# The last attention visits its heads in another order, and the last feed-forward stage runs in two halves of tokens

## Chip, cores and metric

The kernel runs on one NeuronCore of one Trainium2 chip. The metric is the device time of one execution in microseconds (us). Before the change three runs gave 1149.09, 1150.39 and 1150.68 us; the median is 1150.39 us.

## What is computed

Four sequences of 512 tokens with 256 features go through four layers:

```
L0: h = ln(x);  x1 = x + attention(h) @ Wo;  x2 = x1 + gelu(ln(x1) @ W1) @ W2
    x = x + gate * (x2 - x)                   16 heads of 16 features, causal
L1: a small adapter (256 -> 64 -> 64 -> 256), the middle weight chosen per sequence, then ln
L2: r = x + gelu(x @ Wi[e]) @ Wo[e]; x = ln(r)  weights chosen per sequence
L3: x = ln(x) * (1 + scale) + shift
    x = x + softmax(q k' / 4 + bias, masked) v @ Wo     bias: 16 x 512 x 512 per sequence
    out = x + (g * sigmoid(1.702 g)) @ W2,  g = ln(x) @ W1 + b1
```

Everything is float32, except that the scores are matmuls of bfloat16 parts.

## The kernel before

**Attentions and units.** There are eight attentions (`ATTENTIONS`, L70), each a sequence and a layer. The last one, number 7, is layer L3 of sequence 3. An attention has 64 units; a unit is one head with one tile of 128 query tokens. `unit(U)` (L521) says which: the first 32 units are heads 0 to 7 with query tiles 0, 1, 2, 3 in turn (eight units a tile), the other 32 are heads 8 to 15 with the same four tiles. Sixteen units make a batch: eight heads, two query tiles.

**Ticks.** All engines run through the same count of ticks `U`; each engine's program is a loop over ticks written out at build time. On tick U the tensor engine (PE) computes the scores of unit U (`scores`, L1402), then turns the probabilities of unit U-2 by four transposes (`turn`, L1427), and every fourth tick multiplies four turned units by the values (`values`, L1436). The vector engine (DVE) copies turned probabilities of unit U-3 out of PSUM unless the scalar engine (ACT) does (`ON_ACT`, a table that `copy_sides` at L306 makes from planned loads), and adds the bias and takes the row maximum of unit U (`maxima`, L1164, the instruction at L1178). ACT takes the exponential of unit U in place (L854), with the row sums. Sixteen units after the start of a batch the row sums are inverted (DVE, tick 17 of the batch), spread over partitions (PE, tick 21; ACT copy, tick 22, L870) and the batch's context is normalized into `ctxn` (DVE, tick 23, L1205).

**Dense stages beside attention.** Everything else is planned as events at a tick, an engine and a step (`at`, L92; `BESIDE`, L206); an engine does the events of a tick after its attention work of that tick. `plan_out` (L150) is the output projection: on PE `project` (L1306), two halves of two token tiles each, on DVE `residual` (L1126). `plan_norm` (L96) is a layer norm: `stats`, thirteen short `rsqrt` steps put between the attention work, `apply`. `block3` (L192) is the feed-forward of layer L3: `turn_tokens` (8 transposes), `feature_half` (ACT and DVE, 512 columns each), eight `hidden` steps on PE of two matmuls with 512 columns (L1326) and a gelu each on ACT (L901), then four `ff_out` steps of eight matmuls with 256 columns (L1337), `ff_add` on DVE (L1143) and the store (L915, from ACT's queue).

**The end of the kernel.** After the last attention there is nothing left to run beside. The line `[(9, norm(6), 3), (15, block3, 3)]` and `OUTPUT_AT` 8 put the projection of attention 7 at ticks 72 and 73 of it (it has units up to tick 63), the norm at 73 to 78, and the feed-forward from tick 79 on. Because heads 8 to 15 come last for every query tile, no token has all its heads before the last batch is normalized, at tick 71.

**Queues.** SP's queue issues, in the order written out, the bias loads (512 KB for two units, six pairs in a ring, L555), the weight loads, and the stacks of q and k parts (L567, L569: six transfers for eight heads; `STACKS_AT` puts those of heads 8 to 15 of attention 7 at its tick 4). GpSimd (POOL) loads and converts the mask of a query tile when its first unit is near (L830 to L836), adds the mask to a bias pair when PE has much planned beside it (`mask_sides`, L337; else PE adds it with one more matmul, L1416), and adds b2 to the residual stream (`res_l3`, L794).

Of the kernel before, what the change touches and what calls it, by code (L numbers as in the profile page):

```python
# [71 lines left out]
ALL_UNITS = UNITS * len(ATTENTIONS)  # L72
BIASED = {a: n for n, a in enumerate(a for a, (_, l) in enumerate(ATTENTIONS) if l == 1)}
# [125 lines left out]
def norm(k):  # L199
# [5 lines left out]
STACKS_AT = [(-2, 11)] + [(-28, 4)] * 2 + [(-20, 4)] + [(-28, 4)] * 3 + [(-20, 4)]  # L205
# [9 lines left out]
    [(9, norm(6), 3), (15, block3, 3)],  # L215
]
OUTPUT_AT = [None, 8, 8, 20, 8, 8, 8, 8, 8]
# [18 lines left out]

# [8 lines left out]
def plan_loads():  # L246

    ffns = sorted((first_tick("pe", "hidden", s, f), s, f) for s in range(B) for f in range(3))
    for n, (_, s, f) in enumerate(ffns):
        if n:  # L250
            _, s0, f0 = ffns[n - 1]
            at(last_tick("pe", "hidden", s0, f0) + 1, "sp", "w1", s, f)
            at(last_tick("pe", "ff_out", s0, f0) + 1, "sp", "w2", s, f)
        else:
            at(0, "sp", "w1", s, f)
            at(0, "sp", "w2", s, f)
    at(1, "sp", "expert", 0)
# [21 lines left out]
def order(engine, step, key):  # L279
# [4 lines left out]
    for _, _, k in found:  # L284
# [4 lines left out]
TURN = order("pe", "turn_tokens", lambda a: a)  # L289
NTH = {(s, k): sum(1 for x in TURN if x[1] == k and TURN[x] < n) for (s, k), n in TURN.items()}  # L290
FFN = order("pe", "hidden", lambda a: a[:2])
QKV = order("pe", "qk", lambda a: a[:2])
# [3 lines left out]
              for t0, sf in sorted((t, a[:2]) for t, e, st, a in EVENTS if e == "pe" and st == "hidden" and a[2] == 0)}  # L296
ADAPT = order("pe", "down", lambda a: a[0])
# [65 lines left out]
def build(nc, T, out):  # L363
    with ExitStack() as ctx:
# [175 lines left out]
        def res_count(s, layer):  # L540

            name, n = {0: ("res_l0", 2), 2: ("res_l2", 1), 3: ("res_l3", 1)}[layer]
            total = 0
            for _, _, step, args in sorted((t, i, st, a) for i, (t, e, st, a) in enumerate(EVENTS)
                                           if e == "p" and st.startswith("res")):
                total += NT * (2 if step == "res_l0" else 1)
                if step == name and args[0] == s:
                    return total
# [25 lines left out]
        def _(sp):  # L574
# [45 lines left out]

            def bias_first():
# [14 lines left out]
            def rows(s):  # L636
# [8 lines left out]
                for j, name in enumerate(["L2_cond_bo", "L2_cond_gamma", "L2_cond_beta"]):  # L645
# [5 lines left out]
                  "expert": expert, "rows": rows, "bias_first": bias_first}  # L651
            sp.wait_ge(idx_in, 32)
            for U in range(FIRST, LAST + 1):
# [4 lines left out]
                for step, args in steps.get(U, []):  # L658
                    do[step](*args)

        @block.gpsimd
        def _(pool):
# [136 lines left out]

            def mask_load(m):
# [24 lines left out]
            steps, do = dense_steps("p"), {"res_l0": res_l0, "res_l2": res_l2, "res_l3": res_l3}  # L826
            for U in range(FIRST, LAST + 1):

                V = U + MASK_AHEAD
                if 0 <= V < ALL_UNITS and V // UNITS in BIASED and V % 2 == 0:  # L830
                    _, _, c, t, e, j, _, _ = unit(V)
                    if c == 0 and e == 0 and j == 0:
# [11 lines left out]
        def _(act):  # L844
# [35 lines left out]

            def hi(s, l, i):
# [12 lines left out]
            def gelu(s, f, j):  # L894
# [3 lines left out]
                if f == 1 and j == 0:  # L898
# [3 lines left out]
                               bias=b1[f][:, j:j + 1]).then_inc(g_done, 1)  # L902

# [27 lines left out]
            do = {"feature_half": feature_half, "stack": lambda s, l, c: stack(act, s, l, c), "hi": hi, "mid": mid, "gelu": gelu, "down": down, "expert": expert,  # L931
# [22 lines left out]
            act.wait_ge(stored, 16 * B)  # L954
# [3 lines left out]
        def _(v):  # L958
# [70 lines left out]
            def rsqrt(s, k, i):  # L1029
# [4 lines left out]
                if i == 0:  # L1034
                    for t in range(NT):
                        count[0] += 1
                        ins = v.bn_aggr(mv[:, t, :], stats[:, t, :])
                        if t < NT - 1:
                            ins.then_inc(vec, 1)
# [59 lines left out]

            def rest_of(s, l, i):  # L1100
# [107 lines left out]
            do = {"stats": stats_of, "rsqrt": rsqrt, "apply": apply, "apply_late": apply_late,  # L1208
# [32 lines left out]
        def _(pe):  # L1241
# [27 lines left out]

            def hT_ready(s, k):  # L1270
# [35 lines left out]
            def project(s, l, i):  # L1306
                if i == 0:
# [7 lines left out]
                if i == 1:  # L1315
# [14 lines left out]
            def ff_out(s, f, t):  # L1330
                n = FFN[s, f]
# [70 lines left out]
            def scores(U):  # L1402
# [4 lines left out]
                if U == 2 * HH or U % (UNITS // 2) == 0 and U:  # L1407
# [54 lines left out]
            do = {"turn_tokens": turn_tokens, "qk": qk, "v": v_rows, "project": project, "hidden": hidden,  # L1462
# [24 lines left out]
FF_OUT_BANK = (1, 2)  # L1487
UP_BANK = (2, 0)
# [37 lines left out]
```

## Time and profile before

| what | value |
|---|---|
| median of three runs | 1150.39 us |
| the profiled execution, its own time | 1148.26 us |
| its span, first to last instruction | 1146.2 us |
| mean granted clock of PE, share of full | 0.979 |
| PE, DVE, ACT busy share of the span | 87%, 61%, 61% |

All positions below are microseconds from the span's start. The span ends at 1146.2; the profiled execution took 2.06 us more than its span. "Busy" of PE is modelled from pipelined matmuls. A float32 matmul with 256 or 512 columns leaves two records, a transpose one.

### The profile page before, as it was taken

The numbers are of one execution on the slowest core, as the hardware profiler recorded it, in microseconds if no ns is written. First come the engines' busy times: TensorE is split into PE (matmuls) and PEld (weight loads), VectorE is DVE, ScalarE is ACT, GpSimd is POOL, SyncE is SP. The second block draws the span as 40 slices with busy tenths as digits, with TensorE's granted clock in tenths as the row PEclk, the third lists the DMA queues.
The fourth block names the chain that finished last, engine by engine and source line by source line (L and its number), as shares of the span: only waits on it lengthen the run. The fifth ranks groups of instructions, "written<-read, shape, count | busy, mean of one in ns | idle before, by whom it ended". The sixth has DMA issues, their size and how long they took to land.

```text
span 1146.2 us, 22123 instructions
## 1 busy us (share of the span) xinstructions
PE 1001.6 (87%) x7746; PEld 663.6 (58%) x7834; DVE 703.7 (61%) x1964; ACT 694.9 (61%) x1608; POOL 235.7 (21%) x362
## 2 busy tenths in 40 slices
PE   4878889798889898899789899899897999899868
PEld 3445556455546566466556476566574657657545
DVE  5668773745855747945772757746738764764750
ACT  3556665673765765675665757676656775675731
POOL 8300020000320240530040000630720170080000
PEclk9889999998999999999999999999999999999989
DMA  6878425115162454854735128667385487944500
GB/s 170 222 161 199 75 74 111 39 47 102 36 140 75 90 174 129 187 200 125 143 94 113 38 93 182 206 179 195 113 204 171 139 204 234 230 138 174 176 1 18
DMA packets 118351, 154.78 MB, mean 135 GB/s; under 512 B 12956, under 2 KB 80924, under 8 KB 118244
## 3 DMA queue, kind: packets, MB, share of 16 engines
q1 hardware_dynamic: 113636, 147.04, 48.3%
q0 software_dynamic: 1936, 3.97, 1.3%
q10 hardware_dynamic: 2672, 2.36, 0.6%
q8 instruction: 64, 1.05, 0.4%
q14 instruction: 43, 0.35, 0.1%
HBM read 134.47 MB, written 18.88 MB: 134 GB/s over the span
## 4 chain that ended last, share of the span: by engine, by line
PE 54%; DVE 19%; ACT 16%; issue 10%; DMA 0%; DVEq 0%; ACTq 0%
PE bank L1337 15%; PE bank L1326 9%; PE bank L1433 8%; PE bank L1288 5%; PE bank L1447 5%; PE bank L1412 3%; DVE mrow L1169 3%; DVE bias L1178 3%; ACT gT L901 3%; ACT bias L854 3%; PE bank L1302 2%; ACT prob L851 2%; PE bank L1312 2%; ACT L901 2%; ACT pT L862 2%
## 5 line engine op out<-in xcount | busy, mean ns | idle before, releaser
L854 ACT ACTIVATE bias<-bias,mrow 128x512 f32<-128x512 f32 x256 | 184.0, 719 | 191.6 <-DVE mrow L1178 189.5
L1178 DVE CUSTOM_DVE_ANT_0 bias<-bank,bias 128x512 f32<-128x512 f32 x256 | 175.5, 687 | 195.9 <-PE bank L1412 91.6
L851 ACT ACTIVATE prob<-bank,mrow 128x128 f32<-128x128 f32 (+3 forms) x256 | 134.9, 528 | 194.6 <-DVE mrow L1169 193.1
L1169 DVE TENSOR_REDUCE mrow<-bank 128x1 f32<-128x128 f32 (+3 forms) x256 | 124.1, 486 | 169.0 <-PE bank L1418 167.8
L1433 PE MATMUL bank<-ident,bias 128*128 128x128 f32 x1024 | 157.5, 277 | 37.4 <-ACT pT L862 29.5
L1433 PEld LDWEIGHTS bank<-ident,bias 128*128 128x128 f32 x1024 | 122.2, 142 | 111.3 <-ACT bias L854 56.8
L1326 PE MATMUL bank<-hT,w 128*128 128x512 f32 x384 | 181.7, 604 | 1.3 <-ACT hT L878 1.0
L1412 PE MATMUL bank<-ks,qs 128*128 128x512 bf16 (+3 forms) x425 | 143.5, 338 | 40.1 <-ACT prob L851 34.5
L1337 PE MATMUL bank<-w,gT 128*128 128x256 f32 x768 | 174.3, 381 | 0.0
L1337 PEld LDWEIGHTS bank<-w,gT 128*128 128x128 f32 x768 | 142.5, 190 | 20.2 <-issue 2.7
L821 POOL TENSOR_TENSOR bias<-bias,negmask 128x256 f32<-128x256 f32 x180 | 118.4, 690 | 127.0 <-DMA bias<-in_fside_Bx16xSxS 124.7
L862 ACT ACTIVATE pT<-bank 128x512 f32<-128x512 f32 (+3 forms) x275 | 140.1, 509 | 0.9 <-PE bank L1433 0.9
L1186 DVE COPY pT<-bank 128x512 f32<-128x512 f32 (+3 forms) x237 | 136.3, 575 | 6.1 <-PE bank L1433 5.4
L1433 PE MATMUL bank<-ident,prob 128*128 128x128 f32 x640 | 117.2, 282 | 14.4 <-ACT pT L862 9.0
L1447 PE MATMUL bank<-pT,va 128*32 128x128 f32 x3328 | 119.2, 279 | 3.8 <-DVE ctxn L1205 2.8
L1412 PEld LDWEIGHTS bank<-ks,qs 128*128 128x128 bf16 x512 | 50.1, 98 | 117.9 <-ACT prob L851 65.0
L1326 PEld LDWEIGHTS bank<-hT,w 128*128 128x128 f32 x384 | 67.9, 193 | 60.2 <-issue 58.4
L1447 PEld LDWEIGHTS bank<-pT,va 128*32 128x32 f32 x3328 | 84.5, 110 | 25.7 <-issue 23.7
L1433 PEld LDWEIGHTS bank<-ident,prob 128*128 128x128 f32 x640 | 70.5, 144 | 39.3 <-issue 29.7
L780 POOL TENSOR_TENSOR x<-x,xy 128x256 f32<-128x256 f32 x16 | 13.0, 842 | 314.0 <-DVE h L1066 314.0
L1416 PE MATMUL bank<-negmask,identb 128*128 128x512 bf16 x165 | 62.8, 381 | 6.9 <-issue 2.2
L901 ACT ACTIVATE gT<-bank,b 128x512 f32<-128x512 f32 x96 | 60.0, 686 | 10.2 <-PE bank L1326 9.8
(157 smaller groups left out, 1136.5 us busy)
## 6 DMA issues: line engine op xcount, KB each, us to landing
bias<-in_fside_Bx16xSxS SPq DMA_DIRECT2D x128, 512.0 KB, 4.3
w<-in_L_cond_W SPq DMA_DIRECT2D x16, 1024.0 KB, 5.4
qs<-q_parts SPq DMA_DIRECT2D x30, 384.0 KB, 10.4
ks<-k_parts SPq DMA_DIRECT2D x30, 384.0 KB, 12.0
q_parts<-parts SPq DMA_DIRECT2D x80, 128.0 KB
k_parts<-parts SPq DMA_DIRECT2D x48, 128.0 KB
w<-in_L_cond_Wi SPq DMA_DIRECT2D x4, 1024.0 KB, 4.9
w<-in_L_cond_Wo SPq DMA_DIRECT2D x4, 1024.0 KB, 5.6
```

The lines of the kernel that those rows point to most:

```text
L821: pool.tensor_tensor(b_n, b_n, negmask[:, t, keys], ALU.add).then_inc(masked, 1)
L851: act.activation(prob_of(U), score_bank[U % 2][:, 0:n], ACT.Exp, bias=mrow[:, U % ROW_RING:U % ROW_RING + 1], accum_out=rsum[:, U % ROW_RI ...
L854: act.activation(prob_of(U), prob_of(U), ACT.Exp, scale=-1.0, bias=mrow[:, U % ROW_RING:U % ROW_RING + 1], accum_out=rsum[:, U % ROW_RING: ...
L862: act.activation(pT[:, U % PT_RING, 0:n // P, :], turn_bank[U % 2][:, 0:n].rearrange("p (k q) -> p k q", q=P), ACT.Identity).then_inc(pt_a, 1)
L1169: v.tensor_reduce(m, score_bank[U % 2][:, 0:n], AX_X, ALU.max, negate=True).then_inc(max_done, 1)
L1178: v.tensor_tensor_reduce(out=prob_of(U), in0=score_bank[U % 2][:], in1=prob_of(U), scale=-1.0, scalar=3e38, op0=ALU.add, op1=ALU.min, accu ...
L1186: v.tensor_copy(pT[:, U % PT_RING, 0:n // P, :], turn_bank[U % 2][:, 0:n].rearrange("p (k q) -> p k q", q=P)).then_inc(pt_v, 1)
L1326: mm = pe.matmul(dense_bank[FF_BANK[j]][:], w1[:, c, j * P:(j + 1) * P], hT[:, c, :], start=c == 0, stop=c == ND - 1)
L1337: mm = pe.matmul(dense_bank[FF_OUT_BANK[t // 2]][:, (t % 2) * D:(t % 2 + 1) * D], gT[:, j, t * P:(t + 1) * P], w2[:, j, :], start=j == 0, ...
L1412: mm = pe.matmul(score_bank[U % 2][:, 0:n], qs[:, hd, t * P:(t + 1) * P], ks[:, hd, 0:n], start=True, stop=l == 1 and not on_pe)
L1433: mm = pe.transpose(turn_bank[U % 2][:, k * P:(k + 1) * P], prob_of(U)[:, k * P:(k + 1) * P], ident[:])
L1447: mm = pe.matmul(ctx_bank[32 * j:32 * (j + 1), t % 2 * P:(t % 2 + 1) * P], v_h, pT[:, (GH * w + j) % PT_RING, k, :], start=e == 0 and k == ...
```

## The change

1. **Order of units.** In attention 7 the batches come as (heads 0-7, tiles 0-1), (heads 8-15, tiles 0-1), (heads 8-15, tiles 2-3), (heads 0-7, tiles 2-3): `LAST_ORDER`. So the token tiles 0 and 1 have all their heads after unit 31. The stack of heads 8 to 15 moves from tick 4 to tick 1, the waits for it from unit 32 to unit 16, and POOL's mask work for tiles 2 and 3 to the units 32 and 40.
2. **The last stage in halves.** `plan_half` replaces `plan_out`, `norm(6)` and `block3` for sequence 3. It runs once for token tiles 0 and 1 from tick 40 on, and once for tiles 2 and 3 from tick 72 on: `project` of the half, `residual`, `stats`, `rsqrt` with 2 instead of 4 aggregations (13 steps each time), `apply`, four transposes (`turn_half`), features of 256 columns, and eight hidden steps of two matmuls with 256 columns. Two chunks of hidden features share a PSUM bank (`HALF_BANK`).
3. **Gelus.** For the first half six hidden steps stand at ticks 50, 51, 52, 54, 55 and 56, their six gelus of 256 columns at tick 66, after the last exponential. Hidden steps 6 and 7 stand at tick 73, their gelus at 74. A gelu waits for both chunks of its bank.
4. **The end.** `last_out` writes to the two score banks and a turn bank; `ff_out` for tiles 0 and 1 stands at ticks 73 and 74, for 2 and 3 at 86 and 87. Tiles 2 and 3 are added and stored one by one. The stores of sequence 3 go through SP's queue.

```diff
+LAST_ATT = len(ATTENTIONS) - 1
+LAST_SEQ = ATTENTIONS[LAST_ATT][0]
+HALF = S // 2
+LAST_ORDER = [(0, 0), (1, 0), (1, 2), (0, 2)]
+HALF_AT = [40, 72]
...
+def plan_half(t, s, i):
+
+    at(t, "pe", "project", s, 1, i)
+    at(t + 1, "v", "residual", s, 1, i)
+    at(t + 2, "v", "stats", s, 6, i)
+    for r in range(RSQRT_STEPS):
+        at(t + 3 + r // SLOTS, f"v{r % SLOTS}", "rsqrt", s, 6, r, i)
+    at(t + 6, "v", "apply", s, 6, i)
+    at(t + 7, "p", "res_l3_half", s, i)
+    at(t + 7, "pe", "turn_half", s, i)
+    at(t + 8, "v", "feature_cols", s, i)
+    at(t + 8, "a", "feature_cols", s, i)
+    t += 10
+    ahead = (0, 0, 1, 1, 2, 2, 3, 3) if i else (0, 1, 2, 4, 5, 6, 23, 23)
+    behind = (1, 1, 2, 2, 3, 3, 4, 4) if i else (16, 16, 16, 16, 16, 16, 24, 24)
+    for j, (dt, da) in enumerate(zip(ahead, behind)):
+        at(t + dt, "pe", "hidden_cols", s, i, j)
+        at(t + da, "a", "gelu_cols", s, i, j)
+    if i == 0:
+        t = UNITS * LAST_ATT + HALF_AT[1]
+        for x in range(2):
+            at(t + 1 + x, "pe", "ff_out", s, 2, x)
+        at(t + 9, "v", "ff_add", s, 2, 0)
+        at(t + 10, "sp", "store_part", s, 0)
+    else:
+        for x in range(2):
+            at(t + 4 + x, "pe", "ff_out", s, 2, 2 + x)
+            at(t + 5 + x, "v", "ff_add", s, 2, 1 + x)
+            at(t + 6 + x, "sp", "store_part", s, 1 + x)
...
-STACKS_AT = [(-2, 11)] + [(-28, 4)] * 2 + [(-20, 4)] + [(-28, 4)] * 3 + [(-20, 4)]
+STACKS_AT = [(-2, 11)] + [(-28, 4)] * 2 + [(-20, 4)] + [(-28, 4)] * 3 + [(-20, 1)]
...
-    [(9, norm(6), 3), (15, block3, 3)],
...
-V_LOAD = {"stats": 8, "rsqrt": 2, "apply": 9, "apply_late": 9, "feature_half": 7, "rest": 8, "lo": 8, "v": 8, "residual": 14,
+V_LOAD = {"stats": 8, "rsqrt": 2, "apply": 9, "apply_late": 9, "feature_half": 7, "feature_cols": 4, "rest": 8, "lo": 8, "v": 8, "residual": 14,
...
-A_LOAD = {"feature_half": 7, "hi": 7, "mid": 7, "gelu": 10, "down": 20, "expert": 6}
+A_LOAD = {"feature_half": 7, "feature_cols": 4, "hi": 7, "mid": 7, "gelu": 10, "gelu_cols": 8, "down": 20, "expert": 6}
...
+            if a == LAST_ATT:
+                c, t = LAST_ORDER[u // BATCH][0], LAST_ORDER[u // BATCH][1] + u // (2 * GH) % 2
...
+        last_bank = [score_bank[0], score_bank[1], turn_bank[0]]
...
+            def store_part(s, i):
+                sp.wait_ge(ff_done, 2 * FFN[s, 2] + i + 1)
+                tt = LAST_TILES[i]
+                sp.dma_start(out[s].rearrange("(t p) d -> p t d", p=P)[:, tt, :], xy[s][:, tt, :]).then_inc(stored, 16)
...
+            def gelu_cols(s, i, j):
+                n, cols = FFN[s, 2], slice(HALF * i, HALF * (i + 1))
+                act.wait_ge(f1_psum, NF * (n + i) + (j | 1) + 1)
+                act.activation(gT[:, j, cols], dense_bank[HALF_BANK[j // 2]][:, j % 2 * HALF:(j % 2 + 1) * HALF], ACT.Gelu_apprx_sigmoid,
+                               bias=b1[2][:, j:j + 1]).then_inc(g_done, 1)
...
+            def turn_half(s, i):
+
+                dense_banks_free(issued)
+                pe.wait_ge(wo_done, 2 * LAST_ATT + i + 1)
+                for t in (2 * i, 2 * i + 1):
+                    pe.wait_ge(tok[5], NT * NTH[s, 5] + t + 1)
+                    for c in range(ND):
+                        mm = pe.transpose(dense_bank[c][:, t * P:(t + 1) * P], h[:, t, c * P:(c + 1) * P], ident[:])
+                mm.then_inc(t_psum, 1)
...
+            def hidden_cols(s, i, j):
+                n, cols = FFN[s, 2], slice(HALF * i, HALF * (i + 1))
+                if j == 0:
+                    pe.wait_ge(hT_a, TURN[s, 5] + 1 + i)
+                    pe.wait_ge(hT_v, TURN[s, 5] + 1 + i)
+                    pe.wait_ge(w1_in, 16 * (n + 1))
+                if j == 6:
+                    pe.wait_ge(g_done, NF * (n + i) + 2)
+                for c in range(ND):
+                    mm = pe.matmul(dense_bank[HALF_BANK[j // 2]][:, j % 2 * HALF:(j % 2 + 1) * HALF], w1[:, c, j * P:(j + 1) * P], hT[:, c, cols],
+                                   start=c == 0, stop=c == ND - 1)
+                mm.then_inc(f1_psum, 1)
+
+            def last_out(s, t):
+
+                n, i = FFN[s, 2], max(t - 1, 0)
+                if t == 0:
+                    pe.wait_ge(w2_in, 16 * (n + 1))
+                    pe.wait_ge(max_done, ALL_UNITS)
+                    copied(ALL_UNITS)
+                for j in range(NF):
+                    if t % 2 == 0:
+                        pe.wait_ge(g_done, NF * (n + t // 2) + j + 1)
+                    mm = pe.matmul(last_bank[i][:, (t == 1) * D:((t == 1) + 1) * D],
+                                   gT[:, j, t * P:(t + 1) * P], w2[:, j, :], start=j == 0, stop=j == NF - 1)
+                if t:
+                    mm.then_inc(f2_psum, 1)
...
             def project(s, l, i):
-                if i == 0:
+                if ATT[s, l] == LAST_ATT:
+                    dense_banks_free(issued)
+                    if i:
+                        pe.wait_ge(g_done, NF * FFN[s, 2] + 6)
+                    pe.wait_ge(ctx_norm, BATCHES * LAST_ATT + 2 * (i + 1))
+                elif i == 0:
...
+HALF_BANK = (2, 0, 1, 2)
+LAST_TILES = [slice(0, 2), slice(2, 3), slice(3, 4)]
```

## Rows read from the trace of the kernel before

**Rows 1.** The page: the span, and PE's busy time, share and instructions.

```profile
span 1146.2 us, 22123 instructions
PE 1001.6 (87%) x7746; PEld 663.6 (58%) x7834; DVE 703.7 (61%) x1964; ACT 694.9 (61%) x1608; POOL 235.7 (21%) x362
```

**Rows 2.** Chain that ended last, after the last attention: start us, us, what.

```profile
1099.31 0.43 DVE ctxn L1205
...
1099.88 1.98 PE bank L1312 x8
...
1101.88 0.70 DVE xy L1131
...
1109.58 1.96 PE bank L1266 x8
...
1112.47 15.75 PE bank L1326 x32
1128.22 13.83 PE bank L1337 x64
...
1142.14 0.69 DVE xy L1143
```

**Rows 3.** Windows: length, busy time (records) by engine, PEclk, DMA share, GB/s.

```profile
989.57:1010.47 20.90, 17.66 (x180) 12.53 (x182) 16.46 (x54) 13.74 (x33) 6.08 (x9) 1.00 0.92 223
1010.47:1033.05 22.58, 21.66 (x139) 11.78 (x140) 12.21 (x29) 17.35 (x30) 18.99 (x30) 1.00 0.37 115
...
1053.25:1093.79 40.54, 35.04 (x401) 24.45 (x406) 30.62 (x84) 29.99 (x77) 0.00 (x0) 1.00 0.59 186
...
1099.74:1146.20 46.46, 35.19 (x120) 23.35 (x120) 10.09 (x31) 7.56 (x10) 2.77 (x4) 0.89 0.03 12
...
1105.00:1106.00 1.00, 0.00 (x0) 0.00 (x0) 0.97 (x3) 0.00 (x0) 0.00 (x0) 0.91 0.00 0
1106.00:1107.00 1.00, 0.00 (x0) 0.00 (x0) 0.90 (x7) 0.00 (x0) 0.00 (x0) 0.50 0.00 0
...
1116.00:1117.00 1.00, 1.00 (x4) 0.50 (x3) 0.00 (x0) 0.69 (x1) 0.00 (x0) 0.97 0.00 0
```

**Rows 4.** Line L1178 in 1053.2:1094.2: ns min/median/max, first and last start.

```profile
L1178 DVE CUSTOM_DVE_ANT_0 bias<-bank,bias x31: 678/684/692, 1053.2 to 1093.8; 128x512 f32<-128x512 f32 x31
```

**Rows 5.** Timeline of DVE, attention 7, maxima of units 9, 10 and 11.

```profile
993.27 0.69 DVE L1178 CUSTOM_DVE_ANT_0 bias<-bank,bias 128x512 f32<-128x512 f32 x1 [3.01 <-PE bank L1416]
...
996.00 0.67 DVE L1178 CUSTOM_DVE_ANT_0 bias<-bank,bias 128x512 f32<-128x512 f32 x1
...
999.33 0.68 DVE L1178 CUSTOM_DVE_ANT_0 bias<-bank,bias 128x512 f32<-128x512 f32 x1
```

**Rows 6.** Timeline of ACT and PE: a gelu group, then the attention's end.

```profile
1015.59 1.28 ACT L901 ACT_TABLE_LOAD   x1
1016.88 1.85 ACT L901 ACTIVATE gT<-bank,b 128x512 f32<-128x512 f32 x3
...
1095.23 0.58 ACT L862 ACTIVATE pT<-bank 128x512 f32<-128x512 f32 x1
...
1096.66 0.60 ACT L862 ACTIVATE pT<-bank 128x512 f32<-128x512 f32 x1 [0.86 <-PE bank L1433]
...
1098.89 0.38 ACT L870 ACTIVATE spread<-bank 128x256 f32<-128x256 f32 x1 [1.63 <-PE bank L1458]
...
1099.88 3.69 PE L1312 MATMUL bank<-wo,ctxn 128*128 128x256 f32 x16 [1.02 <-DVE ctxn L1205]
...
1111.56 0.78 ACT L878 ACTIVATE hT<-bank,norm_all 128x512 f32<-128x512 f32 x1 [12.29 <-PE bank L1266]
```

**Rows 7.** DMA issues near 987 and at the end: count, KB, us to landing.

```profile
bias<-in_fside_Bx16xSxS SPq DMA_DIRECT2D x1, 512.0 KB, 14.2
ks<-k_parts SPq DMA_DIRECT2D x1, 384.0 KB, 12.4
...
out<-xy ACTq DMA_DIRECT2D x1, 512.0 KB, 2.9
```

More of the change, by code:

```diff
@@ L246, in plan_loads @@
 def plan_loads():
-    ffns = sorted((first_tick("pe", "hidden", s, f), s, f) for s in range(B) for f in range(3))
+    ffns = sorted((first_tick("pe", "hidden_cols" if (s, f) == (LAST_SEQ, 2) else "hidden", *((s,) if (s, f) == (LAST_SEQ, 2) else (s, f))), s, f)
+                  for s in range(B) for f in range(3))
     for n, (_, s, f) in enumerate(ffns):
@@ L289 @@
 TURN = order("pe", "turn_tokens", lambda a: a)
+TURN[LAST_SEQ, 5] = len(TURN)
 NTH = {(s, k): sum(1 for x in TURN if x[1] == k and TURN[x] < n) for (s, k), n in TURN.items()}
+NTH[LAST_SEQ, 5] = sum(1 for x in TURN if x[1] == 5) - 1
 FFN = order("pe", "hidden", lambda a: a[:2])
+FFN[LAST_SEQ, 2] = len(FFN)
 QKV = order("pe", "qk", lambda a: a[:2])
@@ L545, in res_count @@
                                            if e == "p" and st.startswith("res")):
-                total += NT * (2 if step == "res_l0" else 1)
+                total += {"res_l0": 2 * NT, "res_l3_half": NT // 2}.get(step, NT)
                 if step == name and args[0] == s:
+                    return total
+                if step == "res_l3_half" and (s, layer) == (LAST_SEQ, 3) and args[1] == half:
                     return total
@@ L799, in res_l3, with res_l3_half @@
                 res_landed()
+            def res_l3_half(s, i):
+                pool.wait_ge(tok[5], NT * NTH[s, 5] + 2 * (i + 1))
+                for t in (2 * i, 2 * i + 1):
+                    res(pool.tensor_tensor(xy[s][:, t, :], xy[s][:, t, :], b2[1][:], ALU.add))
+                res_landed()
             def mask_load(m):
@@ L830, in _ @@
                 if 0 <= V < ALL_UNITS and V // UNITS in BIASED and V % 2 == 0:
-                    _, _, c, t, e, j, _, _ = unit(V)
-                    if c == 0 and e == 0 and j == 0:
+                    a, _, c, t, e, j, _, _ = unit(V)
+                    if e == 0 and j == 0 and (c, t) in ([(0, 0), (0, 1), (1, 2), (1, 3)] if a == LAST_ATT else [(0, x) for x in range(NT)]):
                         if BIASED[V // UNITS]:
@@ L1027, in _, with rsqrt @@
             chain = [0]
-            def rsqrt(s, k, i):
+            def rsqrt(s, k, i, half=None):
                 var, bits, guess, sq = nwt[:, 0, :], nwt[:, 1, :], rstd, nwt[:, 2, :]
@@ L1034, in rsqrt @@
                 if i == 0:
-                    for t in range(NT):
+                    tiles = range(NT) if half is None else range(2 * half, 2 * half + 2)
+                    for t in tiles:
                         count[0] += 1
                         ins = v.bn_aggr(mv[:, t, :], stats[:, t, :])
-                        if t < NT - 1:
+                        if t < tiles[-1]:
                             ins.then_inc(vec, 1)
@@ L1207, in _ @@
             steps = dense_steps("v")
-            do = {"stats": stats_of, "rsqrt": rsqrt, "apply": apply, "apply_late": apply_late,
+            do = {"stats": stats_of, "feature_cols": feature_cols, "rsqrt": rsqrt, "apply": apply, "apply_late": apply_late,
                   "feature_half": feature_half, "rest": rest_of, "lo": lo, "v": values_out, "residual": residual,
```

45 lines of the change are left out of this document (33 added, 12 removed).

## The prediction

> **What bounds the kernel now.** I read the page first: PE is busy 87% of the span [rows 1], so in most of the kernel PE time is kernel time. Then the chain of waits from its end backwards, because the change touches only attention 7 and what follows. It shows a tail: the last context is normalized at 1099.74, and the kernel ends at 1146.2, 46.46 us later, in which nothing runs beside anything [rows 2, 3]. Three things stand in that tail one behind the other: PE's own work (projection, turn, hidden 15.75, output 13.83), a stretch of DVE alone from the first residual (1101.88) to the turn (1109.58), and the store. PE is busy 35.19 of the 46.46 us. The clock is in it too: PE works until 1103.57 (3.69 from 1099.88 [rows 6]), idles for DVE until 1109.58, and its granted clock goes from 1.00 to 0.50 in that gap and is back only at 1116 [rows 3]: the lower level, 1.2 instead of 2.4 GHz.
>
> Next, the windows by stage in attention 7, to learn what work costs when it is put beside attention. Undisturbed, from 1053.25 to 1093.79, 31 maxima start, that is 30 ticks in 40.54 us: 1.35 us a tick [rows 3, 4]. PE is busy 35.04 of it, DVE 30.62, ACT 29.99: PE idles 0.18 us a tick and no engine is full; what sets the tick is the round of scores, maximum, exponential, turn. Ticks 8 to 17 carry a whole projection, norm and turn of another sequence: 20.90 us for 10 ticks, 7.4 over 13.5. Ticks 18 to 26 carry eight whole hidden steps with eight gelus: 22.58 us for 9, 10.4 over 12.2 [rows 3].
>
> **The tail after the change.** I build it from the last normalization. Matmuls with 256 columns: 64 records of L1337 in 13.83 us, two records each, 0.432 us a matmul [rows 2].
> - wait for `ctxn` 0.14 (1099.74 to 1099.88 [rows 2]);
> - projection of the second half, 4 matmuls: half of 3.69, 1.85 [rows 6];
> - hidden steps 6 and 7 of the first half, 4 matmuls: 1.73;
> - output of tiles 0 and 1, 16 matmuls: 6.91. Beside these 8.6 us DVE does the second half's residual, norm and apply. Before, both halves took 7.7 (1101.88 to 1109.58 [rows 2]); one half is less than that, so it is ready and its stall is gone. Gelus 6 and 7 have six matmuls (2.6 us) to hide behind;
> - turn of the half, 4 transposes: 8 took 1.96 at the 0.50 clock [rows 2, 3], so 0.5, taken 0.6 with the start;
> - features of 256 columns: a stall of PE. 512 columns took 0.78, the 256-column copy 0.38 [rows 6]; 0.5 plus 0.15 to pass it on, 0.65;
> - eight hidden steps, 16 matmuls: 6.91; gelus follow pair by pair on an otherwise free ACT;
> - output of tiles 2 and 3, 16 matmuls: 6.91;
> - add of 256 columns: 0.5 with its waits (0.69 for 512, 0.43 for the normalization's 256 [rows 2]);
> - store: 3.37 now, from 1142.83 to 1146.2, with 2.9 to landing for 512 KB [rows 2, 7]. A quarter of the bytes: between 1 and 3.4, taken 2.3. Tiles 0 to 2 are stored under matmuls.
>
> Sum 28.5. The clock should stay at 1.00 in all of it, as PE has work without a long pause.
>
> In front of it stands ACT's new batch: one table load and six gelus at tick 66, before the spread copy of tick 70, which releases the last normalization. In the old kernel ACT made copies at 1095.23 and 1096.66 and the spread copy at 1098.89 to 1099.27 [rows 6]. With the planned load of the gelus, `copy_sides` gives the very last copy to DVE (worked through from its formula: 14 of the copies from unit 38 on change sides, unit 63 among them), so ACT is free at 1095.8. Table load 1.28; three gelus of 512 columns took 1.85 [rows 6], 0.6 each, so six of 256 lie between 1.8 and 3.7; with 0.38 each, 2.3. End 1099.4, the spread copy 0.5 later than before; with the upper end and a last copy still on ACT it would be 3.4. I take 0.6. DVE's copy of unit 63 costs 0.1, within it.
>
> - Norm part, ticks 40 to 48. From the old ticks 8 to 10 [rows 3, 5]: the tick with one projection half lasted 3.70, so 2.35 over; the tick with residual and stats of one half (996.00 to 999.33) 3.33, 1.98 over, of which I take 1.7 since the copies there go to ACT. The rsqrt ticks were no longer than others (7.4 less ticks 8 to 10's 5.7 leaves 1.7 for rsqrt, apply of four tiles, turn and features). Half of that last is 0.85, less what slack takes back: 0.2. Sum 4.2. Bounds: half of the whole stage, 3.7, and the whole, 7.4.
> - Hidden part, ticks 50 to 56. The old stage cost 10.4 for 16 matmuls of 0.86, 13.8 us of PE: 0.76 per us of PE. 0.76 x 5.2 = 3.9. PE's idle time of 0.18 x 7 ticks says the same (5.2 - 1.3). There are no gelus and no table loads beside it, which speaks for less: lower bound 2; upper, six eighths of 10.4, 7.8.
> - Masks: the planner's table of PE loads doesn't know the new steps, so PE keeps its mask matmuls in these ticks; that is the state of the undisturbed ticks and adds nothing.
> - The stack of heads 8-15 goes out some 5.7 us earlier. Its last transfer took 12.4 us to land [rows 7]; it is wanted at unit 16, some 28 us after tick 1. What it pushes back is bias loads: the first behind the stack took 14.2 instead of the usual 4 [rows 7]; that one will be the pair of units 10 and 11, issued at about 981.7 and landed at 995.9, wanted at 996.00 [rows 5]. Between 0 and 2; 0.5.
> - POOL's mask work and `res_l3_half` have a free engine; the first half's weights come as before: 0.
>
> Sum 8.6. **Net 17.4 - 8.6 = 8.8 us less.** The profiled execution would go from 1148.26 to 1139.5 (span 1137.4). It lies 2.1 below the median of the runs; from that median, 1150.39, the forecast is **1141.6 us**.
>
> **Rivals.**
> 1. *Attention swallows more.* PE idles 0.18 us a tick; over the 18 ticks 40 to 57 that is 3.2 of the 7.6 us added. Then attention pays 4.4 rather than 8.1, and the time is 1137.9. For it: no gelus beside the hidden steps. Against: the old stages cost 0.76 per us of PE and DVE is loaded as well.
> 2. *The gelu batch holds the spread copy, and the clock falls in the gap.* With 3.4 rather than 0.6 PE would stand from 1098.86 to about 1103.3. The old gap of 6 us cost the clock 6.5 us at half speed after its end (1109.58 to 1116), 3.2 us of work [rows 2, 3]. Together 6.0: 1147.6. The Trainium skill (TensorE: Matmul & The Clock Gate, "Why this matters for your kernels") warns against idle gaps between matmul bursts; the trace agrees for the 6 us gap, and shows a full clock across the 1.0 us one before 1099.88. Against: the last copy leaves ACT.
> 3. *Slower: each stop costs its worst.* The mechanism is that PE works its ticks in order: a dense piece between turn and next scores delays both units in flight, whatever its columns. Eight pieces (projection, turn, six hidden) at the worst measured, 2.35, are 18.8; with residual and stats at 1.98, 20.8, and the time is 1150.39 + 20.8 - 17.4 = 1153.8. It decides once ticks 40 to 63 last over 31.1 + 17.4 = 48.5 us. Against: whole hidden steps with 1.7 us of PE cost only 1.3 each on average.
> 4. *The change doesn't do what it says:* the first half isn't through by tick 63, since each step waits for the one before across engines, and PE stands in front of a wait. The distance of apply and turn is one tick, as in the old norm, which worked in ticks 8 to 17. If the six hidden steps waited instead of filling, about their 5.2 us would come back: 1146.8.
>
> **How the numbers follow.** The forecast 0.63, its own range 1138.5 to 1145; rival 1, 0.12; rival 2, 0.11; rival 3, 0.05; rival 4, 0.05; 0.04 for a sum that cancels (attention at both its upper bounds, 15.2 us: 1148.7). Leaving out rival 3 and part of 1 and 2, the range is 1136.8 to 1147.2. A difference under 0.2% (2.3 us) can't be told from none in this kernel; only rival 3 is over 1152.7, and the cancelling sum with part of rival 3 lies within. Faster 0.91, same 0.05, slower 0.04.
>
> **What would show it.** In the profile after: from the last `ctxn` to the end some 28.5 us with the clock at 1.00; one table load in ACT's last batch, the spread copy within 1 us of the last transposes of the sums; ticks 40 to 63 in some 39 us (31.1 + 8.1); the first maximum of unit 10 waiting little; no wait of PE at the second turn. The forecast is wrong if the ticks with one short hidden step last over 2.4 us each, if PE waits over 3 us for the last `ctxn`, or if the clock falls after 1095.

## The result and the profile after

The changed kernel takes 1140.5 us (median of four runs, 1138.92 to 1140.99) against 1150.54 for the kernel before, measured beside it: 10.0 us less, ratio 0.9911, interval 0.9894 to 0.9929. The forecast was 1141.6. The profiled execution took 1140.81 us, its span is 1138.7.

The page of the kernel after, the line that answers to [rows 1]: PE's work is the same, its share a little higher.

```profile
PE 1001.3 (88%) x7778; PEld 669.2 (59%) x7866; DVE 704.7 (62%) x1975; ACT 698.0 (61%) x1620; POOL 235.3 (21%) x362
```

Windows of the kernel after, in the columns of [rows 3]: ticks 8 to 18, 40 to 50, 50 to 58 of attention 7 (from the maximum of one unit to that of another), and the last normalization to the end.

```profile
991.11:1013.95 22.84, 18.18 (x181) 12.58 (x183) 17.44 (x54) 13.88 (x33) 7.31 (x12) 1.00 0.78 213
1065.09:1082.66 17.57, 15.61 (x171) 11.18 (x173) 13.23 (x47) 13.19 (x32) 1.42 (x2) 1.00 0.54 167
1082.66:1096.94 14.28, 14.17 (x135) 10.85 (x137) 8.15 (x22) 8.28 (x20) 0.00 (x0) 1.00 0.33 109
1110.13:1138.70 28.57, 25.09 (x116) 21.61 (x116) 7.08 (x24) 4.76 (x11) 1.41 (x2) 1.00 0.06 19
```

The first and the last row answer to rows of [rows 3]: 20.90 has become 22.84, 46.46 has become 28.57, and the clock of the tail 1.00 instead of 0.89. The whole difference of the two spans, taken from the starts of the maxima:

| stretch | before | after | difference |
|---|---|---|---|
| start to attention 7, unit 0 | 978.90 | 980.44 | +1.54 |
| ticks 0 to 8 | 10.67 | 10.67 | 0 |
| ticks 8 to 18 | 20.90 | 22.84 | +1.94 |
| ticks 18 to 40 | 51.42 | 51.14 | -0.28 |
| ticks 40 to 50 | 14.78 | 17.57 | +2.79 |
| ticks 50 to 58 | 10.64 | 14.28 | +3.64 |
| ticks 58 to 63 | 6.48 | 6.81 | +0.33 |
| maximum of unit 63 to end of last normalization | 5.94 | 6.36 | +0.42 |
| last normalization to end | 46.47 | 28.59 | -17.88 |
| span | 1146.2 | 1138.7 | -7.5 |

The first line is not the change's: up to attention 7 the plan is the same, and over all profiles of this study unit 0 starts between 978.1 and 983.6. Without it the two profiles differ by 9.0 us, as the medians roughly do. So from here on the stages are compared rather than spans. From tick 40 on, a stage that an edit doesn't touch repeats to 0.1 us where the clock is the same. Ticks 8 to 18 don't repeat when the stack goes out at tick 1: they took 22.16 to 24.32 us in the eight profiles of such kernels, against 20.22 to 20.90 in the five with the stack at tick 4.

The chain of waits of the kernel after, its last 33 us (start us, us, what), where [rows 2] showed the old tail:

```profile
1105.79 1.28 ACT L975
...
1107.46 1.93 ACT gT L975 x5
1109.38 0.28 ACT spread L932
1109.67 0.02 issue
1109.69 0.44 DVE ctxn L1289
1110.13 0.14 issue
1110.26 1.97 PE bank L1440 x8
1112.23 1.73 PE bank L1374 x8
1113.95 6.91 PE bank L1388 x32
1120.86 0.45 PE bank L1361 x4
1121.31 0.02 issue
1121.34 0.57 ACT hT L946
1121.91 0.07 issue
1121.98 7.14 PE bank L1374 x32
1129.13 6.92 PE bank L1388 x32
...
1136.17 0.42 DVE xy L1227
```

DVE's norm has vanished from the chain: it runs from 1112.3 to 1117.9 beside PE's work. One table load and the gelus stand right in front of the spread copy. From 1110.26 to 1136.05 the chain is PE but for the 0.7 us of the features; the last add and the store follow.

### The profile page after: what moved, and what is told of

Read it like the earlier page. It is cut to its first block, busy times and chain, and to the rows that moved or that the text cites. A ratio compares the mean times of both kernels' runs of the same rounds, so it can differ in the third digit from the quotient of the medians.

```text
span 1138.7 us, 22222 instructions
## 1 busy us (share of the span) xinstructions
PE 1001.3 (88%) x7778; PEld 669.2 (59%) x7866; DVE 704.7 (62%) x1975; ACT 698.0 (61%) x1620; POOL 235.3 (21%) x362
## 4 chain that ended last, share of the span: by engine, by line
PE 54%; DVE 18%; ACT 16%; issue 10%; DMA 2%; POOL 1%; ACTq 0%; DVEq 0%; POOLq 0%
PE bank L1467 14%; PE bank L1563 8%; PE bank L1454 7%; PE bank L1577 5%; PE bank L1411 5%; PE bank L1542 3%; DVE mrow L1253 3%; DVE bias L1262 3%; ACT gT L969 3%; ACT bias L916 3%; PE bank L1425 2%; ACT prob L913 2%; PE bank L1440 2%; ACT L969 2%; PE bank L1546 2%
## 5 line engine op out<-in xcount | busy, mean ns | idle before, releaser
L1454 PE MATMUL bank<-hT,w 128*128 128x512 f32 x352 | 166.3, 600 | 0.7 <-issue 0.6
L1467 PE MATMUL bank<-w,gT 128*128 128x256 f32 x704 | 160.4, 381 | 0.0
L1467 PEld LDWEIGHTS bank<-w,gT 128*128 128x128 f32 x704 | 130.3, 190 | 18.1 <-issue 2.2
L1454 PEld LDWEIGHTS bank<-hT,w 128*128 128x128 f32 x352 | 61.3, 192 | 51.1 <-issue 50.7
L1548 PE MATMUL bank<-causal,identb 128*128 128x128 bf16 x256 | 57.4, 225 | 2.5 <-ACT prob L913 1.1
```

The lines of the kernel that those rows point to most:

```text
L1454: mm = pe.matmul(dense_bank[FF_BANK[j]][:], w1[:, c, j * P:(j + 1) * P], hT[:, c, :], start=c == 0, stop=c == ND - 1)
L1467: mm = pe.matmul(dense_bank[FF_OUT_BANK[t // 2]][:, (t % 2) * D:(t % 2 + 1) * D], gT[:, j, t * P:(t + 1) * P], w2[:, j, :], start=j == 0, ...
```

## The experiments

Most are the changed kernel with one edit. The first is the kernel before with one part of the change, and halves_after, best and best_mask have several edits. `...` in a diff marks what is left out. The times of one kernel scatter by several us (the six of stack_tick4 lie between 1136.12 and 1144.54), so a difference of medians below some 3 us is no evidence by itself; what an edit does is read from the stages.

**order_only.** The kernel before, with `LAST_ORDER` in `unit` and `normalize`, the early stack, and POOL's masks.

```diff
+LAST_ORDER = [(0, 0), (1, 0), (1, 2), (0, 2)]
-... + [(-20, 4)]
+... + [(-20, 1)]
+            if a == LAST_ATT:
+                c, t = LAST_ORDER[u // BATCH][0], LAST_ORDER[u // BATCH][1] + u // (2 * GH) % 2
...
```

> The kernel before with nothing of the change but the order of units in attention 7, the stack of heads 8-15 at tick 1 and POOL's mask work moved with it; the old tail stays. Theory: the order itself costs nothing, the early stack pushes bias loads back, so ticks 9 to 17 of attention 7 take 1.7 us more than before, as they do in the changed kernel; total +1.7 us. Rival: those 1.7 us come from something else in the changed kernel (its plan of copies, code layout); then attention 7 lasts as long as before and the time is the same.

Measured: 1152.34 us, ratio 1.0027 (1.0010 to 1.0043) to the kernel before. Its window of ticks 8 to 18, and DVE's maximum of unit 10 in its timeline with the idle time before it:

```profile
991.45:1014.36 22.91, 18.21 (x181) 12.61 (x183) 17.43 (x53) 13.88 (x33) 7.33 (x12) 1.00 0.75 211
```

```profile
999.01 0.69 DVE L1182 CUSTOM_DVE_ANT_0 bias<-bank,bias 128x512 f32<-128x512 f32 x1 [1.04 <-DMA bias<-in_fside_Bx16xSxS]
```

The order by itself costs nothing (ticks 40 to 50 take 14.80, 50 to 58 take 10.64, as before); ticks 8 to 18 take 2.0 us more, of which 0.3 comes back by tick 40 (51.13 instead of 51.42 for ticks 18 to 40). That leaves the expected 1.7. DVE waits for the bias of unit 10, and that transfer took 15.5 us to land. This run has the order and the early stack together; the next one tells them apart.

**stack_tick4.**

```diff
-STACKS_AT = ... + [(-20, 1)]
+STACKS_AT = ... + [(-20, 4)]
```

> The changed kernel with the stack of heads 8-15 of attention 7 back at tick 4. Theory: bias loads of units 8 to 13 are out before it, the wait for the bias of unit 10 (0.95 us) goes, and the stack still lands before unit 16: ticks 9 to 17 get 1.7 us shorter, total 1.2 to 1.7 us less than the changed kernel. Rival: the transfers of 2 MB are late in either place: then unit 16 waits for the stack or another unit for its bias, and the time is that of the changed kernel or 1 us more.

Measured: 1139.61 us, ratio 0.9912 (0.9882 to 0.9942) to the kernel before, which can't be told from the changed kernel's. Window of ticks 8 to 18, and the maximum of unit 10, now without a wait:

```profile
992.08:1012.58 20.50, 17.50 (x180) 12.56 (x182) 16.05 (x53) 13.75 (x33) 5.59 (x8) 1.00 0.93 227
```

```profile
998.52 0.67 DVE L1262 CUSTOM_DVE_ANT_0 bias<-bank,bias 128x512 f32<-128x512 f32 x1
```

22.84 has become 20.50, and unit 16 doesn't wait for the stack. Ticks 18 to 40 take 0.34 more (51.48 instead of 51.14), so 2.0 us are left at tick 40. The early place of the stack was not needed: it cost 2 us and bought nothing. The bias transfer behind the stack takes about as long to land as in the kernel before (14.4 and 14.2 us), but at this place no unit waits for it.

**hidden_after.**

```diff
-    ahead = ... else (0, 1, 2, 4, 5, 6, 23, 23)
-    behind = ... else (16, 16, 16, 16, 16, 16, 24, 24)
+    ahead = ... else (22, 22, 22, 22, 22, 22, 23, 23)
+    behind = ... else (22, 22, 22, 22, 22, 22, 24, 24)
```

> The changed kernel with the six hidden steps of the first half moved from ticks 50-56 to tick 72, behind the attention, their gelus behind them. Theory (a step beside attention costs 0.76 us per us of PE, 4.0 measured for 5.2): attention 7 gets 4.0 us shorter from tick 50 on, the tail 5.2 us longer plus some 0.5 for the wait on the last gelus, less 0.4 for the spread copy that no longer waits: total +1.3 us. Rival 1 (PE idle time swallows steps of 0.86 us nearly whole, and the 4 us come from elsewhere): +4 to +5. Rival 2 (a stop costs its worst, more than its PE time): faster, -1 or less.

Measured: 1142.43 us, 1.9 over the changed kernel, ratio 0.9926 (0.9902 to 0.9950) to the kernel before. Windows of ticks 50 to 58 and of the tail:

```profile
1083.73:1095.20 11.47, 9.28 (x111) 6.76 (x114) 7.96 (x22) 8.06 (x20) 0.00 (x0) 1.00 0.42 135
1107.91:1141.80 33.89, 29.40 (x136) 25.06 (x135) 7.08 (x25) 8.13 (x18) 1.41 (x2) 1.00 0.05 16
```

Attention gets back 2.81 us (14.28 less 11.47), the tail pays 5.30, the spread copy gives 0.47: 2.0 in these stages, and both rivals are out. This profile's ticks 8 to 18 took 24.32 instead of 22.84, with a wait of 2.41 us for the bias of unit 10, which is the early stack's scatter and not the edit's. Moving out six steps with 5.2 us of PE returns 2.8: 0.54 per us, not 0.76. But ticks 50 to 58 are not back at the 10.64 of the kernel before. The other 0.83 lies in ticks 54 to 58, where the copies of units 52 to 57 are on other sides than before the change, and PE waits for one of them:

```profile
1091.77 0.63 PE L1563 MATMUL bank<-ident,bias 128*128 128x128 f32 x4 [0.88 <-ACT pT L924]
```

The sides weren't tried alone.

**halves_after.** Old order of units and `HALF_AT = [72, 92]`, the stack at tick 4 with the old waits and mask work, the first half's hidden steps and gelus in pairs like the second's; nothing beside attention 7.

```diff
-LAST_ORDER = [(0, 0), (1, 0), (1, 2), (0, 2)]
-HALF_AT = [40, 72]
+LAST_ORDER = [(0, 0), (0, 2), (1, 0), (1, 2)]
+HALF_AT = [72, 92]
...
```

> Halves of tokens and their PSUM layout, but nothing of them beside attention 7: old order of units, the first half from tick 72 to its hidden steps, the second half's projection behind them, its norm under the output of tiles 0 and 1. Theory: the gain is the work put beside the attention and the norm hidden under the output; against the changed kernel attention 7 is 8.4 us shorter, the tail longer by the first half's projection, turn and hidden steps (7.6 us), by its own exposed norm (about 5.5) and by the clock at half in and behind that gap (2 to 3): total +7 to +8 us over the changed kernel, 1147 to 1149. Rival: halves alone bring the gain, since the second norm is hidden and the clock holds: 1142 or less.

Measured: 1147.76 us, ratio 0.9982 (0.9965 to 0.9999) to the kernel before, 7.3 over the changed one. Its tail, and two slices of 1 us with the clock:

```profile
1099.90:1144.70 44.80, 35.04 (x152) 29.53 (x152) 12.73 (x46) 9.13 (x19) 2.81 (x4) 0.92 0.04 12
```

```profile
1105.00:1106.00 1.00, 0.00 (x0) 0.00 (x0) 0.83 (x6) 0.00 (x0) 0.00 (x0) 0.97 0.00 0
1106.00:1107.00 1.00, 0.00 (x0) 0.00 (x0) 0.82 (x6) 0.00 (x0) 0.00 (x0) 0.50 0.00 0
```

Of the tail's 17.9 us the halves alone bring 1.7: one norm is hidden, the other still stands alone, and the clock falls in that gap as before. The rest comes from the work beside the attention, and that needs the order of units.

**gelu_beside.**

```diff
-    behind = ... else (16, 16, 16, 16, 16, 16, 24, 24)
+    behind = ... else (7, 7, 7, 7, 7, 7, 24, 24)
```

> The changed kernel with the first half's six gelus at tick 57, among the exponentials, instead of tick 66. Theory: ACT stops for two table loads and six gelus, 1.28 + 2.3 + 1.28 = 4.9 us, of which its idle time in these ticks takes 1 to 2; ticks 50 to 63 get 3 to 4 us longer, and 63 to the last normalization 0.4 to 0.5 shorter, since the spread copy no longer waits: total +2.5 to +3.5 us over the changed kernel. Rival: PE is what limits these ticks, ACT has room for the stop, and the total falls by the 0.4 of the spread copy.

Measured: 1146.74 us, 6.2 over the changed kernel, twice what was expected. From its chain of waits:

```profile
1100.42 1.28 ACT L975
1101.71 0.01 issue
1101.72 2.30 ACT gT L975 x6
1104.02 0.02 issue
1104.03 1.28 ACT L916
```

Ticks 58 to 63 take 11.50 instead of 6.81, 4.7 us for a stop of 4.9: ACT's idle time takes next to nothing of it. The part about the spread copy was wrong too: 63 to the last normalization takes 6.89, not 5.9. The spread copy no longer waits for the gelus, but PE's sums come 6.0 us after the maximum of unit 63 instead of 5.0: the planner moved six of the last ten copies to the other engine, and PE waits 1.12 us for one on ACT. So this run changed more than the place of the gelus, and how much of the 4.7 the moved copies account for is not shown.

**hidden_pairs.**

```diff
-    ahead = ... else (0, 1, 2, 4, 5, 6, 23, 23)
+    ahead = ... else (0, 0, 2, 2, 4, 4, 23, 23)
```

> The changed kernel with its six hidden steps as three pairs at ticks 50, 52 and 54 in place of six single ones. The PE work is the same. Theory: what is paid is PE time over PE's idle time; a pair is as long as a whole step of before, which cost 0.76 us per us, against the 0.54 that moving the single ones out has shown: ticks 50 to 58 take about 1 us more (15.3). Rival (each stop costs, whatever its size): three stops less, ticks 50 to 58 take 1.4 us less (12.9).

Measured: 1140.31 us. Window of ticks 50 to 58:

```profile
1080.31:1094.49 14.18, 13.94 (x133) 10.72 (x135) 7.96 (x22) 8.39 (x20) 0.00 (x0) 1.00 0.33 110
```

14.18 against 14.28: both theories miss. Three pieces or six make no difference; PE is busy 13.94 of the 14.18 us, so what counts there is the sum of its work.

**mask_pool.**

```diff
-PE_LOAD = {..., "hidden": 17, ...
+PE_LOAD = {..., "hidden": 17, "hidden_cols": 17, ...
```

> The changed kernel with hidden steps of the halves in the planner's table of PE loads (17, as for whole ones): POOL, idle there, adds the mask for units 50 to 57, PE does 8 matmuls of 0.22 us less. Theory: the chain of waits runs through PE alone in these ticks, so ticks 50 to 58 get 1.2 to 1.8 us shorter (12.5 to 13.1 instead of 14.3). Rival: the bound there is the round over DVE and ACT, or POOL's four additions per pair come late: 0, or some tenths longer.

Measured: 1140.24 us, nothing gained. Windows of ticks 40 to 50 and 50 to 58:

```profile
1066.53:1085.54 19.01, 15.79 (x171) 11.16 (x173) 14.68 (x47) 13.17 (x32) 7.20 (x12) 1.00 0.49 154
1085.54:1098.51 12.97, 12.64 (x127) 9.86 (x128) 8.13 (x23) 8.16 (x20) 4.46 (x8) 1.00 0.38 122
```

The second is 1.31 shorter, as expected; the first is 1.44 longer. The tail took 30.13 instead of 28.59, for another reason (see the next run). The timeline of DVE (start us, us) and of POOL in tick 43 and after:

```profile
1074.66 0.39 DVE L1117 TENSOR_SCALAR norm_rows_t<-norm_rows_t 128x4 int32<-128x4 int32 x1
1075.09 0.60 DVE L1119 TENSOR_SCALAR norm_rows_t<-norm_rows_t 128x4 int32<-128x4 int32 x1
1075.72 0.58 DVE L1121 TENSOR_TENSOR norm_rows_t<-norm_rows_t 128x4 f32<-128x4 f32 x1
...
1077.66 0.16 DVE L1121 TENSOR_TENSOR norm_rows_t<-norm_rows_t 128x4 f32<-128x4 f32 x1
```

```profile
1074.36 2.56 POOL L883 TENSOR_TENSOR bias<-bias,negmask 128x256 f32<-128x256 f32 x4 [37.67 <-DMA bias<-in_fside_Bx16xSxS]
```

The same instruction on four elements takes 0.58 us while POOL adds and 0.16 behind it. Not every instruction suffers: POOL's next twelve additions ran from 1082.24 to 1090.08, and DVE's maxima (0.69 us) and copies (0.68) in that stretch took what they always take. The Trainium skill (GPSIMD Engine Reference, "Specifications") says that POOL shares its SBUF interfaces with VectorE and contends with instructions that have two SBUF inputs or run in a two-port mode. The slowed steps with two inputs, L1121 and L1123, agree; whether the slowed steps with one input (L1117, L1119) ran in such a mode, no row shows.

**last_copy_act.** One execution only.

```diff
 ON_ACT = copy_sides()
+ON_ACT[ALL_UNITS - 1] = True
```

> The changed kernel with the copy of the last turned unit (63) on ACT, as in the kernel before, in place of DVE. Theory: ACT's batch of table load and six gelus then starts 1.4 us later, and the spread copy and the last normalization with it: from the maximum of unit 63 to the last normalization 7.8 us instead of 6.36, the tail behind it the same 28.6. Rival: the gelus don't hold the spread copy (it waits for PE's sums): 6.4 as now.

Measured: 1142.22 us. From unit 63 to the last normalization it took 7.75 us, as expected; the tail was expected at 28.6 and took 30.4. Of its PE timeline, and of the one of mask_pool, the second projection:

```profile
1110.20 3.22 PE L1441 MATMUL bank<-wo,ctxn 128*128 128x256 f32 x8 [2.89 <-DVE ctxn L1290]
```

```profile
1111.82 3.48 PE L1440 MATMUL bank<-wo,ctxn 128*128 128x256 f32 x8 [1.48 <-DVE ctxn L1289]
```

In the changed kernel's timeline it is:

```profile
1110.26 1.97 PE L1440 MATMUL bank<-wo,ctxn 128*128 128x256 f32 x8 [1.49 <-DVE ctxn L1289]
```

The slices of mask_pool show the clock fall in the gap before it:

```profile
1111.00:1112.00 1.00, 0.18 (x1) 0.21 (x2) 0.42 (x1) 0.22 (x1) 0.00 (x0) 0.74 0.00 0
1112.00:1113.00 1.00, 1.00 (x3) 0.82 (x4) 0.00 (x0) 0.00 (x0) 0.00 (x0) 0.50 0.00 0
```

So a gap of 1.48 us already lost the clock in one profile, and did not in the changed kernel (1.49), nor in stack_tick4 and hidden_pairs (1.49 each). In last_copy_act the clock stood at 1.00 through the whole gap of 2.89 us and fell to 0.50 only after the projection had begun (0.88 in the slice from 1110 to 1111, 0.50 in the next); the expectation below counts it as a fall in the gap.

**gap_filled.**

```diff
-    ahead = ... else (0, 1, 2, 4, 5, 6, 23, 23)
+    ahead = ... else (0, 1, 2, 4, 5, 6, 21, 21)
```

> The changed kernel with hidden steps 6 and 7 of the first half at tick 71, ahead of the second projection, instead of tick 73, behind it. PE stood 1.5 us there for the last normalization; in two of the kernels run so far its granted clock fell to 0.5 in that gap and cost 1.2 to 1.5 us more. Theory: the two steps (1.73 us) fill the gap, the clock stays at 1.00 in every run, and from the last normalization to the end it takes 27.1 instead of 28.6 us: total 1.4 us less than the changed kernel where its clock held, 3 less where it fell. Rival: the steps wait for gelus 0 and 1 behind ACT's batch, and push the projection back by what they take: 0 gained.

Measured: 1140.44 us, ratio 0.9918 (0.9896 to 0.9940): no gain in the medians. In the stage where it acts the gain is there, while in this kernel's profile ticks 8 to 18 waited longer for the bias than in the changed kernel's (23.45 against 22.84). PE's timeline and the tail's window:

```profile
1110.71 0.44 PE L1588 MATMUL bank<-ident,rwide 128*128 128x128 f32 x2
1110.98 1.89 PE L1374 MATMUL bank<-hT,w 128*128 128x256 f32 x8
1112.71 1.89 PE L1440 MATMUL bank<-wo,ctxn 128*128 128x256 f32 x8
```

```profile
1112.48:1139.40 26.92, 23.52 (x110) 20.10 (x108) 7.09 (x25) 4.76 (x11) 1.41 (x2) 1.00 0.06 21
```

26.92 instead of 28.57: the two steps fill the gap, PE goes from the sums through the projection without a pause. The clock holds here; the tails of best and best_mask, filled in the same way, take 26.86 and 26.92. That it holds in every execution is not shown.

**best.** stack_tick4 and gap_filled together.

> Both mends together: stack of heads 8-15 at tick 4, hidden steps 6 and 7 at tick 71. Theory: they act in different places and add up: ticks 8 to 18 in 20.5 to 20.9 us, last normalization to end 27.1, total 3.1 us less than the changed kernel, about 1137.4. Rival: the stack comes late for unit 16 in some executions, and the time scatters with the changed kernel's.

Measured: 1137.9 us (median of six runs), ratio 0.9894 (0.9875 to 0.9914); ticks 8 to 18 in 20.22, the tail 26.86. Against the changed kernel that is 2.6 and 1.7 less, and ticks 18 to 40 take 0.3 more: 4.1 in the stages, while 3.1 was expected and the medians differ by 2.6. The intervals of the two ratios overlap, so the medians alone don't show that this kernel is faster than the changed one.

**best_mask.** best, and POOL adds the mask of units 54 to 57.

```diff
+for _n in (27, 28):
+    ON_PE[BIASED[LAST_ATT] * UNITS // 2 + _n] = False
```

> The kernel with both mends, and POOL in place of PE adding the mask for units 54 to 57 only. In the run with units 50 to 57 the gain of 1.3 us in ticks 50 to 58 was lost in tick 43, where DVE's short norm instructions took 0.39 to 0.60 instead of 0.17 us while POOL added. Theory (the two engines hold each other up): units 54 to 57 have their bias later, POOL adds behind the rsqrt steps, so ticks 40 to 50 last 17.6 as in the changed kernel and ticks 50 to 58 13.6 instead of 14.3; total 0.7 less than with both mends alone. Rival (the slow steps were not POOL's doing, or POOL slows whatever DVE does then): ticks 40 to 50 again over 18.5, no gain.

Measured: 1134.59 us, ratio 0.9868 (0.9849 to 0.9887), the fastest kernel of the study and the only one whose interval lies clear of the changed kernel's on the faster side. Ticks 40 to 50 and 50 to 58:

```profile
1060.73:1078.29 17.56, 15.61 (x171) 11.17 (x173) 13.24 (x46) 13.18 (x32) 4.63 (x8) 1.00 0.52 165
1078.29:1091.71 13.42, 13.31 (x131) 10.40 (x133) 8.21 (x22) 8.16 (x20) 1.91 (x4) 1.00 0.34 117
```

17.56 as in the changed kernel, and 0.86 less behind it. POOL adds from 1075.00 on, behind the short norm steps, and these take 0.16 to 0.17 us again. So the masks on POOL paid where its additions fell behind those steps, and didn't where they fell on them. The medians' further 3.3 us over best is more than the 0.86 that the stages explain. Unit 0 started 1.8 us earlier in this profile than in best's; where that comes from is not shown, and scatter is a guess.

## Why the prediction was right

**In short.** The forecast was 8.8 us less, the stages show 9.0 and the medians 10.0. The tail and its mechanism were right. What attention pays was right in its sum, 8.6 against 8.4, but the norm part was 1.4 too large and the stack 1.2 too small, and that the two cancel is luck.

**The tail: right, term by term.** Forecast 28.5 us from the last normalization, measured 28.57: projection 1.97 (1.85), hidden 1.73 (1.73), output 6.91 and 6.92 (6.91), turn 0.45 (0.6), features 0.67 (0.65), hidden 7.14 (6.91), 0.54 to the end of the add from the last matmul's (0.5), and 2.1 for the store (2.3). The terms that had rows in the same shape were off by less than 0.25; the clock held, as forecast. That it held had some luck in it: the same tail behind the same gap lost it in mask_pool.

**The spread copy: right.** 0.42 later than before, forecast 0.6. The batch went as worked out: table load 1.28 and six gelus 2.3. From the end of ACT's last copy to the first gelu 1.31 us pass (1105.78 to 1107.09), so the switch of tables costs the load alone here. last_copy_act shows what the planner's choice for the last copy was worth, 1.4 us. (The tables of the two kernels differ in 15 copies from unit 38 on, not 14; unit 63 is among them.)

**What attention pays: right in sum, two of three parts mis-sized.** Forecast 8.1 for ticks 40 to 63, measured 6.76; and 0.5 for the stack, measured 1.66 over ticks 8 to 40. The same ticks in the kernel before, 40 to 50 and 50 to 58, with nothing beside them:

```profile
1061.89:1076.67 14.78, 12.91 (x158) 8.82 (x159) 10.42 (x29) 10.57 (x27) 0.00 (x0) 1.00 0.71 195
1076.67:1087.31 10.64, 9.14 (x109) 6.57 (x112) 7.90 (x22) 7.33 (x19) 0.00 (x0) 1.00 0.41 145
```

- The norm part was taken at 4.2 and cost 2.79, below even its stated bound of 3.7. The step that failed is the comparison with a mean tick of 1.35. Ticks differ by their place in the round of values and batches, and these ten take 1.48 each with nothing beside them. Tick 40 alone took 1.88 (maxima of units 40 and 41 in the kernel before, 1061.89 and 1063.77), so the projection cost 1.82 and not 2.35. Against the same places, the whole old stage cost 6.1, and half of that is 3.1. Ticks 40 to 42 together came close (3.8 over, forecast 4.05); the larger miss is behind them, where ticks 43 to 49 took 1.0 less than before while 0.2 more was forecast. Part of that may be the copies that changed sides; it wasn't tried.
- The hidden part was taken at 3.9, and ticks 50 to 58 got 3.64 longer, ticks 58 to 63 another 0.33. PE's busy time there went from 9.14 to 14.17 us, its idle time from 1.50 to 0.11: the steps fill the idle time and pay for the rest. That is the prediction's second way of reckoning (5.2 less 1.3), and it holds. Its first one, 0.76 per us of PE, came from a stage with gelus and table loads, and it fits only by its number: hidden_after gets back 2.8 for the same steps, because ticks without them take 11.47 in the new plan. The 0.33 stays in hidden_after too, so it comes from elsewhere in the plan.
- The stack: the mechanism and the unit were right (the pair of units 10 and 11, a margin of nothing), the size at the upper end of "between 0 and 2". The bias transfer took 14.0 us to land in the changed kernel and 15.5 in order_only, 14.2 in the kernel before. So the delay is about the old one; it now meets a unit that has no time to spare. Over ticks 8 to 40 the eight profiles with the early stack lie 1.0 to 3.3 us above the kernel before, so the 0.5 was too low for each of them.
- The signs. Ticks 40 to 63 took 38.66 us, forecast some 39; but they started from 31.90 in the kernel before and not from 31.1. Ticks 52 and 56, with one short hidden step each, lasted 2.83 and 2.48, over the 2.4 that was to speak against the forecast. Tick 52 took 2.56 without a step, so one mark for all ticks was a poor sign.

**The rivals.** Number 1 (attention swallows more) was partly true: 6.8 lies between its 4.4 and the forecast's 8.1. Its mechanism is seen beside the hidden steps, where PE's idle time is used up, and not beside the norm, where PE idles 1.96 us of ticks 40 to 50 after the change and 1.87 before. Number 2 was real in kind: the clock did fall in the gap before the second projection, in mask_pool with the gap as short as in the changed kernel. Its price there was 1.5 us, against 3.2 for the clock alone in the rival's 6.0: by the slices of 1 us the half clock lasted some 3.4 us (1111.5 to 1114.9). Number 3 is refuted by hidden_pairs, where the number of stops makes no difference; number 4 by ticks 50 to 58, where PE is busy 14.17 of 14.28 us, so the steps fill and don't wait.

## What to carry to other kernels

A stage that stands alone at the end is worth cutting in parts when another order of the work before it lets one part start early; the cut alone brought 1.7 of 17.9 us here. Price what you put beside a running loop against the same place in its round, not its mean, and ask how much idle time of the engine it can fill (1.4 of 5.2 us here). Keep the other engine's table switches out of the loop; the one tried here cost 4.7 us for a stop of 4.9. Then look at the new plan's seams: a transfer moved "to be safe" cost 2 us, and filling a 1.5 us gap of PE gave 1.7, where a fall of the clock behind the same gap had cost 1.5 more.

## What was not expected of the hardware

- Four additions on POOL (2.56 us) stretched DVE's steps on four elements from 0.17 to between 0.39 and 0.60 us, and cost a tick of attention some 1.4 us; additions beside DVE's maxima and copies stretched nothing.
- PE's granted clock fell from 1.00 to 0.50 in a gap of 1.48 us in one execution and held through one of 1.49 in three others; in a fifth it held through 2.89 us and fell behind the gap. What decides isn't visible in these profiles.
- The bias transfer behind the six stack transfers (2 MB) took 13.7 to 15.6 us to land, in all thirteen profiles and with the stack at either tick, instead of 3.3 to 4.2 for those ahead of the stack in the kernel before. Where the stack stands decides only whether a unit waits for it.
